# Cross-attention over 16 batches on one core: a new opening order, and exponentials of two units at once in the last two batches

## The reference

```python
Q = relu(queries @ Wq + bq); K = relu(keys @ Wk + bk); V = relu(values @ Wv + bv)   # values are the keys
# 16 heads of width 8, 16 batches, 100 queries and 1444 keys each, D = 128
scores = einsum('hbqd,hbkd->hbqk', Qh, Kh) / sqrt(8)
scores = where(key_mask == 0, NEG, scores)       # a key whose row sums to 0 is masked
attn = softmax(scores) * q_mask                  # a query whose row sums to 0 gives 0
out = einsum('hbqk,hbkd->hbqd', attn, Vh) -> (B, Sq, D), + queries
```

## Time and profile before

| | |
|---|---|
| median of 3 runs | 360.11 us |
| the profiled execution | 360.41 us |
| its span (first to last instruction) | 358.5 us |
| busy: PE, PEld, DVE, ACT | 349.2, 243.6, 236.6, 300.4 us |
| granted TensorE clock | full (1.00) |
| DMA traffic | 64.55 MB, mean 180 GB/s |

### The profile page before, as it was taken

The page is one execution under the profiler, slowest core; times in us unless marked ns, Lnnn a source line. Parts: engine busy times, 40 slices in busy tenths (PEclk is TensorE's granted clock), DMA queues, the critical chain, the costliest instruction groups (busy, mean ns, idle before and its releaser), DMA issues.

```text
span 358.5 us, 16853 instructions
## 1 busy us (share of the span) xinstructions
PE 349.2 (97%) x6706; PEld 243.6 (68%) x6706; DVE 236.6 (66%) x777; ACT 300.4 (84%) x397; POOL 7.2 (2%) x30
## 2 busy tenths in 40 slices
PE   8899899999999999999999999999999999999994
PEld 5657576776767677676767767676776767677662
DVE  5948887593948659394866839486684939579321
ACT  1488588888989888898989889898988888898993
POOL 6010000000000000000000000000000000000000
PEclk9999999999999999999999999999999999999999
DMA  6658748775664638366463837546373754537000
GB/s 205 218 144 306 241 155 322 225 254 177 232 190 158 195 121 286 92 240 181 168 189 130 273 91 257 165 166 206 135 252 91 275 148 168 176 110 236 10 11 5
DMA packets 40398, 64.55 MB, mean 180 GB/s; under 512 B 28084, under 2 KB 29364, under 8 KB 40372
## 3 DMA queue, kind: packets, MB, share of 16 engines
q1 hardware_dynamic: 39442, 63.26, 55.0%
q10 hardware_dynamic: 930, 0.90, 0.7%
HBM read 13.73 MB, written 0.82 MB: 41 GB/s over the span
## 4 chain that ended last, share of the span: by engine, by line
PE 92%; DVE 4%; DMA 1%; ACT 1%; issue 1%; ACTq 1%; DVEq 0%
PE psum L629 36%; PE psum L605 29%; PE psum L551 13%; PE psum L542 12%; DMA wq_sb<-in_Wq 1%; PE psum L703 1%; DVE k_raw L830 1%; ACT k_parts L502 1%; DVE late_low L1075 0%; ACT probs L511 0%; DVE k_high L849 0%; DVE k_cent L849 0%; PE psum L572 0%; DVE query_bd L902 0%; DVE k_low L854 0%
## 5 line engine op out<-in xcount | busy, mean ns | idle before, releaser
L511 ACT ACTIVATE probs<-psum 121x800 f32<-121x800 f32 x384 | 293.3, 841 | 41.1 <-PE psum L605 41.1
L629 PE MATMUL psum<-probs,values 121*32 121x200 f32 x3072 | 153.6, 333 | 0.0
L629 PEld LDWEIGHTS psum<-probs,values 121*32 121x32 f32 x3072 | 96.0, 110 | 42.1 <-issue 18.7
L605 PEld LDWEIGHTS psum<-query_bd,k_parts 64*121 64x121 f32 x1536 | 91.8, 181 | 45.9 <-issue 40.1
L605 PE MATMUL psum<-query_bd,k_parts 64*121 64x200 f32 x1536 | 115.7, 281 | 1.1 <-ACT k_parts L502 0.9
L830 DVE TENSOR_SCALAR_CACHE_REDUCE k_raw<-psum,bk_sb 128x361 f32<-128x361 f32 (+2 forms) x63 | 37.6, 598 | 80.1 <-PE psum L542 80.1
L551 PE MATMUL psum<-wv_sb,keyT 128*32 128x129 f32 (+1 forms) x1536 | 54.7, 277 | 0.0
L542 PE MATMUL psum<-keyT,wk_mixed 128*32 128x361 f32 (+2 forms) x504 | 52.4, 489 | 1.2 <-DVE k_raw L830 1.2
L883 DVE TENSOR_SCALAR values<-v_biased,keep 121x128 f32<-121x128 f32 x192 | 43.2, 283 | 6.3
L551 PEld LDWEIGHTS psum<-wv_sb,keyT 128*32 128x32 f32 (+1 forms) x1536 | 38.1, 108 | 6.7 <-DMA bv_sb<-in_bv 0.4
L873 DVE TENSOR_TENSOR v_biased<-psum,bv_sb 121x384 f32<-121x384 f32 x64 | 35.0, 548 | 0.0
(11 more groups left out here) (81 smaller groups left out, 78.7 us busy)
## 6 DMA issues: line engine op xcount, KB each, us to landing
k_parts<-k_high SPq DMA_DIRECT2D x30, 722.0 KB, 5.0
k_parts<-k_low SPq DMA_DIRECT2D x30, 722.0 KB, 5.5
keyT<-in_ctxT SPq DMA_DIRECT2D x15, 722.0 KB, 4.3
query_rep<-late_high SPq DMA_DIRECT2D x2, 600.0 KB, 7.7
query_rep<-late_low SPq DMA_DIRECT2D x2, 600.0 KB, 7.8
residual<-in_x SPq DMA_DIRECT2D x64, 12.5 KB
k_parts<-k_high SPq DMA_DIRECT2D x2, 480.0 KB, 3.4
k_parts<-k_low SPq DMA_DIRECT2D x2, 480.0 KB, 3.4
```

Source lines behind the costliest of these rows:

```text
L511: nc.scalar.activation(probs[0:KTILE, u % PROB_SLOTS], scores_ps[0:KTILE, u % SCORE_SLOTS, :, 0:QCOLS], ACT.Exp, scale=SCALE).then_inc(pro ...
L605: mm = nc.tensor.matmul(scores_ps[0:KTILE, u % SCORE_SLOTS, j, n * TCOLS:(n + 1) * TCOLS], k_parts[rows, parity, t, kt * KTILE:(kt + 1) * ...
L629: mm = nc.tensor.matmul(spans[c * VCOLS:(c + 1) * VCOLS, half, :, :, 0:SPAN], values[0:KTILE, parity, kt, half * HALF_PAIRS + c, :], probs ...
```

## The change

Loads and ScalarE's queue: Wq is issued ahead of the first xT; the late xT is issued only when the last chunk of batch 0's keys and the first xT have landed. PE: the first query projection comes behind all three key chunks; `select_keys` comes ahead of values 2 and 3; the scores of units 0 and 1 stand between these, and the projections of groups 1 to 3 come later. ScalarE does the relu of group 1 behind unit 1's exponential and those of groups 2 and 3 behind unit 2's. VectorE: key chunk 0 is read before Wq is mixed, and the keys' maximum and high part come before the first queries' low part; in batch 0 `turn_mask` and `high_queries` go behind the first two reads of batch 1's keys, and `read_keys(2, 0)` ahead of `spread_queries(1)`. `turn_mask` waits for a semaphore of its own in place of four pads. In batches 14 and 15 ScalarE takes the exponential of two units in one instruction (121 x 1600), then of the third alone, in each cycle.

```diff
+    LATE_QUERIES = {1: (1,), 2: (2, 3)}
...
-            nc.gpsimd.memset(flat_mask[:, :, :, SPAN:], 0.0)
+            nc.gpsimd.memset(flat_mask[:, :, :, SPAN:], 0.0).then_inc(mask_padded, 1)
...
+            act.dma_start(wq_sb[:], Wq).then_inc(wq_loaded, 16)
             act.dma_start(xT_sb[:, 0:QB * SQ].rearrange("p (b q) -> p b q", b=QB), xT[:, 0:QB, :]
                           ).then_inc(first_xT_loaded, 16)
-            act.dma_start(wq_sb[:], Wq).then_inc(wq_loaded, 16)
-            act.dma_start(xT_sb[:, QB * SQ:].rearrange("p (b q) -> p b q", q=SQ), xT[:, QB:, :]
-                          ).then_inc(xT_loaded, 16)
...
             nc.scalar.activation(unused[:], ones[:, 0:1], ACT.Exp).then_inc(table_loaded, 1)
+            act.wait_ge(first_keys_loaded[KCHUNKS - 1], 16)
+            act.wait_ge(first_xT_loaded, 16)
+            act.dma_start(xT_sb[:, QB * SQ:].rearrange("p (b q) -> p b q", q=SQ), xT[:, QB:, :]
+                          ).then_inc(xT_loaded, 16)
...
-                    if isinstance(b, int) and b == 0 and u + 1 < QGROUPS:
-                        relu_queries(u + 1)
+                    if isinstance(b, int) and b == 0 and u in LATE_QUERIES:
+                        for g in LATE_QUERIES[u]:
+                            relu_queries(g)
+
+            def batch_by_pairs(b):
+
+                for first in range(0, UNITS, CYCLE):
+                    for u, units in ((first, 2), (first + 2, 1)):
+                        act.wait_ge(scores_ready, UNITS * b + u + units)
+                        act.wait_ge(pv_done, UNITS * b + u + units - PROB_SLOTS)
+                        at, slot = u % PROB_SLOTS, u % SCORE_SLOTS
+                        nc.scalar.activation(probs[0:KTILE, at:at + units], scores_ps[0:KTILE, slot:slot + units, :, 0:QCOLS],
+                                             ACT.Exp, scale=SCALE).then_inc(probs_ready, units)
 
             batch(0, 0)
-            pairs_loop(act, 1, B - 1, batch)
-            batch(B - 1, 1)
+            pairs_loop(act, 1, B - 3, batch)
+            batch(B - 3, 1)
+            batch_by_pairs(B - 2)
+            batch_by_pairs(B - 1)
...
             for c in range(KCHUNKS):
-                if c == KCHUNKS - 1:
-                    pe.wait_ge(wq_permuted, 1)
-                    pe.wait_ge(first_xT_loaded, 16)
-                    project_queries(0)
                 pe.wait_ge(first_keys_loaded[c], 16)
                 project_keys(psum[:, K_BANKS[c], :], 0, c * BANK, min((c + 1) * BANK, SK)).then_inc(first_projected, 1)
+            pe.wait_ge(wq_permuted, 1)
+            pe.wait_ge(first_xT_loaded, 16)
+            project_queries(0)
...
+            select_keys()
             first_values(2)
+            first_scores(0)
             first_values(3)
-            select_keys()
+            first_scores(1)
             pe.wait_ge(xT_loaded, 16)
-            for u in range(LEAD):
-                first_scores(u)
-                if u + 1 == QGROUPS - 1:
-                    pe.wait_ge(q_relued, QGROUPS - 1)
-                project_queries(u + 1)
+            project_queries(1)
+            first_scores(2)
+            project_queries(2)
+            pe.wait_ge(q_relued, QGROUPS - 1)
+            project_queries(3)
             sum_queries(0)
...
                 for c in range(KPARTS):
                     read_keys(1, c, used + c)
+                    if c == 0:
+                        turn_mask()
+                    elif c == 1:
+                        high_queries()
...
+                used = used + VGROUPS
+                read_keys(2, 0, used)
                 dve.wait_ge(mask_step, 1 + QUAD)
                 dve.wait_ge(q_replicated, 16 * SLOTS)
                 spread_queries(1, 1)
-                used = used + VGROUPS
-                read_keys(2, 0, used)
-                turn_mask()
-                high_queries()
                 read_keys(2, 1, used + 1)
...
-                dve.wait_ge(pads_zeroed, 4)
+                dve.wait_ge(mask_padded, 1)
...
-            dve.wait_ge(wq_loaded, 16)
-            mix_columns(wq_mixed, wq_sb, wq_permuted)
             dve.wait_ge(bk_loaded, 16)
             for c in range(KCHUNKS):
                 read_keys(0, c, c, False)
+                if c == 0:
+                    dve.wait_ge(wq_loaded, 16)
+                    mix_columns(wq_mixed, wq_sb, wq_permuted)
+            max_keys(0, KCHUNKS, False)
+            center_keys(k_high, 0, k_high_ready)
             dve.wait_ge(q_relued, 2)
             low_first_queries(slice(0, SQ))
-            max_keys(0, KCHUNKS, False)
-            center_keys(k_high, 0, k_high_ready)
             center_keys(k_cent, 0, k_cent_ready)
```

More of the change, by code:

```diff
@@ L217, in attention @@
         groups_made = sem("groups_made")
+        mask_padded = sem("mask_padded")
         rows_grouped = sem("rows_grouped")
```

## The result

| | before | after |
|---|---|---|
| median of the runs compared | 360.13 us (4 runs, 360.03 to 360.51) | 364.78 us (4 runs, 363.60 to 365.73) |
| ratio | | 1.0128, 95% interval 1.0108 to 1.0147 |
| the profiled execution | 360.41 us | 365.0 us |
| its span | 358.5 us | 363.0 us |

The change makes the kernel 1.3% slower. The forecast was 360.6 us, the range ended at 361.5: both wrong, and by more than any rival gave.

A forecast was written before the change was run, and what follows sets the result against it. It took PE and ScalarE to be both at their limit in the last batches, in a loop through both. Opening +0.87, batch 0 -1.3 and pairs +0.9 summed to +0.5 us: 360.6 us, range 358.8 to 361.5.

The forecast's parts named there:

- Opening: Before cycle 0: first scores 0.81 us sooner, but unit 1's scores wait for VectorE's read; cycle 0 0.87 later.
- Batch 0: VectorE's reorder takes the sixth and seventh cycles from 7.90 to 6.44 us; -1.3 us in all.
- Pairs: Last two batches: a pair takes 1504 ns, but the loop lengthens cycles from 2.20 to 2.28 us; +0.9 us.
- Rival C: Last two batches: ScalarE alone is the bound, 11 pairs save 0.07 to 0.08 each, -0.8 us, 358.9; chance 0.17.
- The Trainium skill's estimate: Paired exponentials in the last batches: each merge saves 93 ns of overhead, -1.0 us over 11 pairs.
- The rest of the run up to 328 is PE's own and moves with it: Between batch 0 and the last two batches: PE's work only shifts with what came before, no term of its own.
- part 4: The working on exponentials by pairs in the last two batches: +0.9 us, ends -0.2 and +1.75.
- Rivals B to E: Four rivals: pairs save nothing, 0.15; ScalarE alone bounds the tail, 0.17; opening's 0.81 is kept, 0.11; nothing much changes, 0.12.
- A: The forecast itself for the whole kernel, 360.6 us, with a spread of 0.5; chance 0.45.
- slower: The outcome that the whole kernel gets slower by over 0.2%, given a chance of 0.30.

The follow-up runs named there:

- e10: The changed kernel without pairs, with the late-xT wait ahead of unit 1's scores (PE one instruction longer); ratio 0.9992 to the kernel before, 359.14 to 361.56 us.
- e15: The kernel before with new load order and VectorE's batch 0 (358.25 us), plus key selection ahead of values 2 and 3; ratio 0.9989, 358.29 to 360.62 us.
- the opening alone: The kernel before with the changed opening only (loads, PE, first reads), VectorE's batch 0 and exponentials as before; ratio 1.0072, 360.36 to 366.04 us.
- e9: The kernel before with the engines' new opening order; loads, VectorE's batch 0 and exponentials as before; ratio 1.0041, 360.84 to 368.42 us.
- e12: The whole changed kernel with the late-xT wait ahead of unit 1's scores (PE one instruction longer); median 361.88 us, ratio 1.0058 to the kernel before.
- one less: The kernel before with only the late-xT wait moved ahead of project_queries(1) (PE one instruction shorter); ratio 1.0027, 359.84 to 364.47 us.

## Why the prediction was wrong

**Opening**: right in its mechanism. The keys were early and gave no more than forecast, the scores of unit 1 waited 1.02 for VectorE, values 3 gave away what was won. +0.87 was put, +0.42 came, and the 0.45 between them gathered in small steps: the selection 0.15 sooner than put (10.85 for 11.00), scores 0 0.25 (15.98 for 16.23), unit 1 0.33 (18.00 for 18.33), cycle 0 0.45 (22.08 for 22.53).

**Batch 0**: -1.3 forecast, -1.35 in the profile, and alone -1.15 by the medians.

**Pairs**: the price was right (1504 ns), and so was the loop, PE's pair of scores to ScalarE and back: 1.50 + 0.05 + 0.77 = 2.32 for 2.29. Rival C had the price too, but not the loop. The Trainium skill's estimate ("ScalarE: Activation LUTs", "What ACT_TABLE_LOAD costs"), 11 x 0.093 saved, fell. Its fixed cost and its price of an element agree with the trace (1519 ns by them for the pair, 1504 measured), its overlap nearly (0.10 here). From the pair's start to the single's are 1.40 to 1.41 us, against 1.47 for two singles, so 0.07 was saved per pair, and the loop gave it all back. The term was small by a third (+0.9 for +1.3), since the cycle was 0.03 longer and some 11 cycles bore it.

**What failed** is the sentence that stands behind batch 0, "The rest of the run up to 328 is PE's own and moves with it", and with it the silence of part 4 on what straight code costs. Both treat an engine's instructions as simply there. What the runs showed in its place are two waits for code: 2.5 us of PE in batch 2 and 1.5 us of ScalarE near the end, 4.0 of the 4.5 us. Opening, batch 0 and the pairs' cycles sum to +0.4, forecast +0.5. Rivals B to E all were about engines and waits; none was about code, though the page before lists an instruction queue with 21 pieces. (A slip beside it: the upper quarter of A's 0.45 is 0.11, so "slower" had 0.26 and not 0.30.)

How sure is it? That moving one wait, and with it one instruction of PE, brings the stall and takes it away is shown from both sides: with one less the kernel before has it, in 4 of 10 executions by their times and in the one profiled; with one more the changed kernel's profile has none, and the median falls by 2.9. All five profiles with 58 semaphore instructions have the stall, none of the eleven with 59. Both edits move the same wait, though; an instruction added or removed elsewhere was not tried, so that it is the length of the program and not the place of this wait is argued. That the wait is for code is read from the trace: no semaphore ends it, and the q8 piece starts only when PE has run dry. The Trainium skill ("Runtime: NRT & Kernel Launch", "Instruction fetch mechanics") says that code comes in blocks of 16 KiB by a queue that the sequencer drives itself, and that the cost at a block's edge is mostly hidden; the trace agrees with the 16 KB of each piece of q8 and has one edge here at which 2.5 to 2.8 us are not hidden. The same section says that a taken branch to code outside the two pages held breaks the sequential prefetch and stalls. No taken branch stands ahead of this stall: PE's first one in the changed kernel's trace is the loop's, at 89.42. Open is why one execution asks for the piece in time and the next one doesn't, with the same program; of the changed kernel's four executions three (364.56 to 365.73) lie above all of those with one instruction more, and the fourth (363.60) lies where that kernel's upper ones do without a stall.

For the clock it is weaker. Half-clock stretches were seen behind PE's stall (two profiles) and at the key selection or soon after it (three); the edit that makes the pause alone brings the upper level in 6 of 10 executions, the kernel without it has none in four. By the rows a stretch costs 1.5 us, while the levels of e10 and of e15 lie 2.0 apart, so 0.5 is not accounted for. Which length of pause, or which work around it, it takes stays open. The changed kernel's profiled execution runs at full clock throughout, so its 4.5 us contain nothing of this; its other executions may.

## What to carry to other kernels

A reorder on an engine also shifts its code. Where a profile shows an idle time of a microsecond or more that ended by "issue" while the other engines wait for this one, look at the instruction queue of the DMA view beside it before anything else, and try the same kernel with one instruction more. Replacing a loop by straight code near the end of a program has a price, here about 1 us on ScalarE, against 0.08 per cycle that the pairs were to save. And the merged instruction did save 0.07 us, but the loop ran through a second engine, where the longer piece waits for more input and frees its slots later: work out that loop first. Last, two parts of this change were good by themselves, and only runs of each part showed it.

## What was unexpected of the hardware

- Moving one semaphore wait, which changes no engine's work and PE's start of cycle 0 by 0.15 us, cost 2.3 to 4.2 us in four of ten executions, 60 us after the place of the edit.
- After a late code piece has landed, PE needs 1.3 to 1.5 us more to go on (80.99 to 82.45 in the changed kernel, 82.25 to 83.56 in "the opening alone"), ScalarE 1.0 to 1.3 (338.23 to 339.24; 352.98 to 354.30).
- Each stretch at 1.2 GHz cost 1.5 us (the key selection and what stands behind it took 1.5 longer in the profiles of e9, e10 and e12 than in the changed kernel's, and it is 1.48 behind the stall of "one less"). They came behind pauses of PE of 1.3 to 2.4 us; behind pauses of 1.26 and 2.20 us in the changed kernel's profile, and of 1.55 in that of e15, the clock stayed full.
- Pairs in a loop with waits on register values had cycles of 2.41, straight ones 2.32.
- Of PE's 21 code pieces none starts after 82.95 and before 296.81 in the kernel before: all turns of PE's loop but the first run without a fetch, so the stall of batch 2 comes once and not in each turn.
